# One graph layer on one core: biases copied into PSUM, projection ahead of the node updates, x added from PSUM, every second edge sum on VectorE

## The chip, the cores and the metric

One core of a Trainium2 chip. The metric is the device time of one execution in microseconds; three runs of a kernel are made and their median is told. The profile is one further execution, with the instructions of all engines.

## What is computed

512 nodes of 1024 features, 8192 edges sorted by destination. With xn = layernorm(x):

```python
feat  = concat([xn[src], xn[dst]])                     # per edge, 2048 wide
e     = relu(feat @ W_kind + b_kind)                   # 256 edges hh, 1280 oo, 6656 ho
logit = e @ W_a + b_a
alpha = exp(logit - segmax[dst]) / segsum[dst]         # softmax over each node's edges
z     = segment_sum(alpha * xn[src], dst)
gnn   = relu([xn, z] @ W_n + b_n)                      # W_hn for nodes 0..127, W_on for the rest
q, k, v = split(xn @ w_qkv + b_qkv); q = elu(q)+1; k = elu(k)+1    # 16 heads of 64
mix   = ((q @ (k^T v)) / (q . sum k)) @ w_proj + b_proj
x     = x + gnn + mix
x     = x + ffn(layernorm(x))                         # two int8/ternary-quantised layers, gelu between
```

Products with fp32 weights are made of three products each, of the parts "hi" (rounded to fp32r) and "lo" (the rest): hi x hi, hi x lo, lo x hi.

## The kernel before

**Chunks.** All weights come as chunks of 1024 x 512 (2 MB), each in two halves of 1 MB. `chunk_product` (L1468) makes one chunk's rows: for each of the two halves, for each row (128 nodes) 4 x 3 products of 128x512 into one PSUM bank. The order of the chunks is the order of everything: `HHT0, HHB0, HHT1, HHB1, K0, HN0, V0, HN1, K1, V1, Q0, Q1, ON0, ON1, PR0, PR1` after eight tables, and behind them BON0, BON1, BHN0, BHN1, which need z. A table is xn @ (half of W_ho or W_oo), four rows, and goes to DRAM; an edge's product is then a row of the source table plus a row of the destination table. HN has one row, ON three, HH two, the others four. The banks 0 to 3 are taken in turn (L402-414); `free` (L1597) waits until the bank's last reader is through.

**Bias.** A chunk in `BIASED` has a row of 512 biases. SP loads it twice (2 KB each) into `b_raw`, ScalarE makes its hi part (L654), VectorE its lo part (L884), and TensorE adds it as one more product with a row of ones, ahead of a bank's first product (`add_bias`, L1454, L1478; `first_chunk`, behind the last). These are 52 products.

**A half of weights** goes: SP loads it into `raw[h]` when VectorE is through with what lay there (`load_next`, L470); ScalarE makes the hi part (`hi_half`, L647), the first half when the chunk before last is done and the second when the first half of the chunk before is; VectorE makes the lo part (`lo_half`, L879). Both hi and lo lie in rings of three halves.

**Edges.** GpSimd gathers 68 tiles of 128 edges (L583-601): the source rows plainly, two thirds of the destination rows with an addition in the DMA; for one tile in three (`ADDED_HERE`) the destination rows go into one of two buffers (`SECOND`), and VectorE adds them (L1057). Eight slots (`SLOTS`) hold rows. `edge_tile` (L1045) on VectorE makes the relu and dot product (L1063), the mask (L1075) and the running maximum (L1087). `TILES` says how many tiles VectorE takes in each chunk, before and after the next chunk's first `lo_half`.

**Attention.** K, V and Q go through ScalarE's `positive_part` and VectorE's `add_kq`; k^T v (`kv_product`), the denominators (`den8`, `invert_den`) and `attend` are made at places of `KV_AT`, `DEN8` and `ATTEND`. Heads 0 to 7 are attended in Q1, heads 8 to 15 in ON0. PR0 and PR1 multiply the result with w_proj; ScalarE copies their banks into one of two staging slots, GpSimd adds x there (L612), SP stores them (`mix_out`).

**After the edges** GpSimd makes the maximum over partitions (L604), then PR's additions, then the lo parts of xn (L615), which ScalarE's `xn_hi` (L785) precedes. VectorE takes 36 of the edge maxima in PR1 (L1185), the exponents, and then for each tile three one-hot matrices (L1242-1244) which TensorE multiplies (L1628, L1629) into a 512 x 512 matrix A. A is transposed, z made, then ON's and HN's second halves, and the last stage with the MLP.

Every engine runs its own list in order, and so does SP, which waits for VectorE ahead of each load and for the reader ahead of each store.

Of the kernel before, what the change touches and what calls it, by code (L numbers as in the profile page):

```python
# [5 lines left out]
F32 = mybir.dt.float32  # L6
# [55 lines left out]
for _c in range(CHUNKS):  # L62
# [14 lines left out]
ADDED_HERE = [t for t in range(T_GATHERED) if t % 3 == 2]  # L77
# [14 lines left out]
ATTEND = {(Q1, 1, 0): [(0, 0), (0, 1)], (Q1, 1, 1): [(0, 2), (0, 3)], (ON0, 1, 0): [(1, 0), (1, 1)], (ON0, 1, 2): [(1, 2), (1, 3)]}  # L92
DEN8 = {(Q1, 0, 2): 0, (ON0, 0, 1): 1}
KV_AT = {(HN1, 0, 0): 0, (Q0, 0, 0): 1}


def build(nc, x, src, dst, wt, bias_rows, bq, w_a, b_a, ln1_g, ln1_b, w1, b1, ln2_g, ln2_b, w2, b2, out):
# [108 lines left out]
    b_raw = sb("b_raw", [P, CW], F32, at_braw)  # L206
# [3 lines left out]
    b_hl = sb("b_hl", [P, 2, CW], F32R, at_bhl)  # L210
# [7 lines left out]
    rz = sb("rz", [P, N], F32, at_braw)[64:72, :]  # L218
    sel8 = sb("sel8", [P, 4, P], F32R, at_bhl)
# [4 lines left out]
    ones_b = sb("ones_b", [64, P], F32R)  # L224
    ones_r = sb("ones_r", [P, P], F32R)
# [58 lines left out]
    bias_hi_done = sem("bias_hi_done")  # L284
    bias_lo_done = sem("bias_lo_done")
# [139 lines left out]
    def _(sp):  # L425
# [31 lines left out]
        sp.wait_ge(dve_consts, 1)  # L457
        load_bias(0)
# [5 lines left out]
        sp.wait_ge(bias_lo_done, 1)  # L464
        load_bias(1)
# [1331 lines left out]
```

## Time and profile before

| | |
|---|---|
| median of 3 runs | 788.03 us (785.34 to 793.8) |
| the profiled execution | 790.62 us, span 788.9 us |
| busy, share of the span | PE 668.7 us (85%), DVE 533.0 (68%), ACT 212.0 (27%), POOL 261.7 (33%) |
| granted TensorE clock, mean | 0.912 |
| DMA | 163.4 MB, 207 GB/s over the span |

PE is TensorE's products, PEld its weight loads, DVE VectorE, ACT ScalarE, POOL GpSimd; SP issues most transfers. Products are pipelined: a product of 512 columns has a row of about 0.39 us, but they start every 0.23 us, so the distance of starts is their price.

### The profile page before, as it was taken

The page shows a single profiled execution, that of the slowest core. Times are in us where ns is not written, and L with a number is a line of the kernel's source. Part 1 is how long each engine was busy: PE and PEld are TensorE (multiplying, and loading weights), DVE is VectorE, ACT ScalarE, POOL GpSimd, SP SyncE. Part 2 cuts the span into 40 slices and gives each one's busy share as a digit, 9 for nine tenths or more (in the row PEclk, how much of TensorE's full clock was granted, in tenths as well). Part 3 has the DMA queues.
Part 4 walks back from the last instruction along what each step waited for, and adds up shares of the span by engine and source line. Part 5 has one row for each costly group of instructions (what it writes and reads, how often), then busy time and mean ns, then how long its engine had stood idle before and what let it go on. Part 6 is the DMA issues. An engine that isn't in the chain of part 4 may idle for free.

```text
span 788.9 us, 8358 instructions
## 1 busy us (share of the span) xinstructions
PE 668.7 (85%) x2739; PEld 469.2 (59%) x2741; DVE 533.0 (68%) x1106; ACT 212.0 (27%) x266; POOL 261.7 (33%) x191
## 2 busy tenths in 40 slices
PE   4999999999989989999999988991917677798952
PEld 3778887788777666877886555761601011586621
DVE  7878814566287876847758676851688887327996
ACT  3232232213322443343352623211220010320101
POOL 3000308475156373736753033614250000002340
PEclk9999999999999998999999989995955768999985
DMA  9544539999989989989999183981450023140202
GB/s 348 215 160 160 184 137 306 365 339 338 332 247 352 354 239 321 298 290 310 323 324 276 55 264 106 321 267 44 156 226 1 0 64 150 54 138 6 107 27 80
DMA packets 41722, 163.40 MB, mean 207 GB/s; under 512 B 5168, under 2 KB 5552, under 8 KB 34512
## 3 DMA queue, kind: packets, MB, share of 16 engines
q0 software_dynamic: 20160, 73.41, 32.0%
q1 hardware_dynamic: 20800, 88.88, 30.2%
q10 hardware_dynamic: 720, 0.59, 0.2%
q8 instruction: 22, 0.36, 0.2%
q14 instruction: 20, 0.16, 0.1%
HBM read 146.08 MB, written 16.78 MB: 206 GB/s over the span
## 4 chain that ended last, share of the span: by engine, by line
PE 45%; DVE 26%; DMA 13%; issue 8%; ACT 3%; DVEq 2%; POOL 2%; SPq 0%; ACTq 0%; POOLq 0%
PE bank_low L1429 12%; PE bank_low L1430 11%; PE bank_low L1431 11%; DMA w_raw<-in_wt 6%; DMA gathered_rows<-edge_tables,src_row 3%; DMA edge_tables<-stage 3%; DVE w_lo L887 3%; DVE gathered_rows L1063 2%; DVEq L1042 2%; DVE hot_hi L1243 2%; DVE hot_src L1242 2%; PE bank_low L1455 2%; DVE hot_lo L1244 2%; PE bank_high L1628 1%; DVE thrown_away L1185 1%
## 5 line engine op out<-in xcount | busy, mean ns | idle before, releaser
L1429 PE MATMUL bank_low<-w_hi,xT_hi 128*128 128x512 f32 x484 | 196.9, 407 | 10.3 <-DVE w_lo L887 7.9
L1430 PE MATMUL bank_low<-w_lo,xT_hi 128*128 128x512 f32 x484 | 191.7, 396 | 0.0
L1431 PE MATMUL bank_low<-w_hi,xT_lo 128*128 128x512 f32 x484 | 191.2, 395 | 0.0
L887 DVE TENSOR_TENSOR w_lo<-w_raw,w_hi 128x2048 fp32r<-128x2048 f32 x48 | 110.0, 2291 | 65.0 <-ACT w_hi L660 63.2
L660 ACT ACTIVATE w_hi<-w_raw 128x2048 fp32r<-128x2048 f32 x49 | 93.7, 1912 | 183.0 <-DMA w_raw<-in_wt 118.5
L1429 PEld LDWEIGHTS bank_low<-w_hi,xT_hi 128*128 128x128 f32 x484 | 92.6, 191 | 39.7 <-issue 12.9
L577 POOL DMA_INDIRECT gathered_rows<-edge_tables,dst_row x46 | 88.9, 1933 | 59.7 <-DMA gathered_rows<-edge_tables,src_row 52.1
L1431 PEld LDWEIGHTS bank_low<-w_hi,xT_lo 128*128 128x128 f32 x484 | 92.7, 192 | 20.0
L577 POOL DMA_INDIRECT gathered_rows<-edge_tables,src_row x68 | 85.1, 1251 | 57.5 <-DVE gathered_rows L1063 20.8
L1430 PEld LDWEIGHTS bank_low<-w_lo,xT_hi 128*128 128x128 f32 x484 | 92.7, 192 | 18.1
L1063 DVE SCALAR_TENSOR_TENSOR gathered_rows<-gathered_rows,wa_bc 128x1024 f32<-128x1024 f32 x68 | 83.4, 1226 | 15.3 <-DMA gathered_rows<-edge_tables,dst_row 13.5
L1628 PE MATMUL bank_high<-hot_src,hot_hi 128*128 128x512 f16 x68 | 36.3, 534 | 41.2 <-DVE hot_lo L1244 32.7
L622 POOL TENSOR_TENSOR small<-small,nhalf 128x1 f32<-128x1 f32 x12 | 10.7, 890 | 169.1 <-DVE small L1323 156.2
L577 POOL DMA_INDIRECT gathered_dst<-edge_tables,dst_row x22 | 28.7, 1306 | 109.6 <-DVE gathered_rows L1057 107.5
L1628 PEld LDWEIGHTS bank_high<-hot_src,hot_hi 128*128 128x128 f16 x68 | 7.1, 104 | 86.1 <-issue 85.9
L683 ACT ACTIVATE stage<-bank_low 128x512 f32<-128x512 f32 x48 | 27.9, 594 | 109.1 <-PE bank_low L1431 41.9
L1455 PE MATMUL bank_low<-b_hl,ones_b 64*128 64x512 f32 x52 | 26.3, 506 | 18.0 <-ACT stage L683 17.9
L1629 PE MATMUL bank_high<-hot_src,hot_lo 128*128 128x512 f16 x68 | 36.6, 539 | 0.0
L1075 DVE TENSOR_SCALAR other_node<-iota,dst_f 128x128 bf16<-128x128 f16 (+1 forms) x70 | 17.9, 257 | 26.1 <-issue 26.0
L1242 DVE TENSOR_SCALAR hot_src<-iota,src_f 128x512 f16<-128x512 f16 x70 | 26.5, 379 | 7.1 <-PE bank_high L1629 6.5
L1455 PEld LDWEIGHTS bank_low<-b_hl,ones_b 64*128 64x128 f32 x52 | 9.6, 185 | 35.9 <-ACT stage L683 19.9
L1087 DVE SCALAR_TENSOR_TENSOR running_max<-other_node,logit,running_max 128x128 bf16 (+1 forms) x70 | 25.2, 360 | 3.6 <-DVE gathered_rows L1063 2.8
(277 smaller groups left out, 1016.2 us busy)
## 6 DMA issues: line engine op xcount, KB each, us to landing
w_raw<-in_wt SPq DMA_DIRECT2D x54, 1024.0 KB, 8.0
edge_tables<-stage SPq DMA_DIRECT2D x32, 256.0 KB, 3.8
x_in<-in_x SPq DMA_DIRECT2D x4, 512.0 KB, 9.1
xn_scratch<-xn SPq DMA_DIRECT2D x4, 512.0 KB, 4.5
node_top<-stage SPq DMA_DIRECT2D x8, 256.0 KB, 2.7
x_part<-in_x SPq DMA_DIRECT2D x8, 256.0 KB, 10.2
mix_out<-stage SPq DMA_DIRECT2D x8, 256.0 KB, 2.0
xn_raw<-xn_scratch SPq DMA_DIRECT2D x4, 512.0 KB, 5.9
```

What stands on the lines that cost most here:

```text
L577: pool.indirect_dma_start(dest, None, table_d[0:nodes, :], bass.IndirectOffsetOnAxis(ap=index[:, t:t + 1].bitcast(U32), axis=0), compute_o ...
L660: act.activation(w_half(c, h)[0], raw[:, h, :], ACT.Copy).then_inc(w_hi_done, 1)
L683: act.activation(stage[:, slot, :], bank[b][:, :], ACT.Copy).then_inc(evac_done, 1)
L887: dve.tensor_tensor(lo, raw[:, h, :], f32(hi), ALU.subtract).then_inc(w_lo_done, 1)
L1063: dve.scalar_tensor_tensor(out=row, in0=row, scalar=0.0, in1=wa_bc[:, :], op0=ALU.max, op1=ALU.mult, accum_out=logit[:, t:t + 1]).then_inc ...
L1242: dve.tensor_scalar(hot_src[:, s, :], iota[:, :], src_f[:, t:t + 1], None, ALU.is_equal).then_inc(hot_done, 1)
L1429: pe.matmul(dest, lh, rh, start=start and i == 0, stop=False)
L1430: pe.matmul(dest, lh, rl, start=False, stop=False)
L1431: last = pe.matmul(dest, ll, rh, start=False, stop=last_one)
L1455: return pe.matmul(bank[b][:, :], ones_b[:, :], b_hl[0:64, bias_no(c) % 2, :], start=start, stop=stop)
L1628: pe.matmul(out, hot_hi[:, t % 2, 0:P], hot_src[:, t % 2, :], start=False, stop=True, skip_group_check=True)
L1629: pe.matmul(out, hot_lo[:, t % 2, 0:P], hot_src[:, t % 2, :], start=False, stop=True, skip_group_check=True).then_inc(hot_used, 1)
```

## The change

- The bias is no product. SP loads the row once, broadcast to 128 partitions (256 KB), and ScalarE copies it into each bank before the chunk's products (`seed`); TensorE's products all accumulate (`start=False`), and `free` waits for `seeded`.
- The chunks' order is now `HHT0, HHB0, HHT1, HHB1, K0, V0, K1, V1, Q0, Q1, HN0, PR0, PR1, HN1, ON0, ON1`. The tables come bottom halves first, and the bias is in the second pair (`WEIGHTS`, `BIAS_ROW`). Heads 8 to 15 are attended in PR0.
- VectorE adds x to PR0's and PR1's banks from PSUM into the staging slots (`add_x`); ScalarE doesn't copy them.
- VectorE adds 34 of 68 tiles instead of 22. `TILES` starts a chunk earlier and ends in PR0; the 36 maxima are taken in ON0 and ON1.
- xn is read back in HN1, and its hi and lo parts are made in ON0 by ScalarE and VectorE. The one-hot loop waits for ON1's banks instead of PR1's.

```diff
+WEIGHTS = [2, 3, 0, 1, 6, 7, 4, 5, 8, 9, 10, 11, 12, 14, 16, 17, 18, 19, 13, 22, 23, 15, 20, 21, 24, 25, 26, 27]
+BIAS_ROW = {2: 0, 3: 1, 6: 2, 7: 3, HHT0: 4, HHT1: 5, K0: 6, HN0: 7, V0: 8, HN1: 9, K1: 10, V1: 11, ON0: 12, ON1: 13, PR0: 14, PR1: 15}
-TILES = {5: (2, 3), 6: (2, 2), 7: (3, 2), HHT0: (1, 1), HHB0: (1, 2), HHT1: (1, 1), HHB1: (1, 1),
-         K0: (3, 2), HN0: (0, 1), V0: (2, 3), HN1: (0, 1), K1: (2, 2), V1: (3, 2), Q0: (2, 3), Q1: (2, 2),
-         ON0: (2, 2), ON1: (1, 2), PR0: (2, 6)}
+TILES = {4: (0, 1), 5: (3, 2), 6: (3, 2), 7: (2, 3), HHT0: (2, 1), HHB0: (1, 1), HHT1: (1, 2), HHB1: (1, 1),
+         K0: (3, 2), V0: (3, 2), K1: (3, 3), V1: (2, 3), Q0: (3, 2), Q1: (5, 2), HN0: (2, 0), PR0: (4, 3)}
-MAXIMA = {PR1: (0, 36)}
+LAST_EDGES = PR0
+MAXIMA = {ON0: (0, 18), ON1: (18, 36)}
-ADDED_HERE = [t for t in range(T_GATHERED) if t % 3 == 2]
+ADDED_HERE = [t for t in range(T_GATHERED) if t % 2]
-ATTEND = {(Q1, 1, 0): [(0, 0), (0, 1)], (Q1, 1, 1): [(0, 2), (0, 3)], (ON0, 1, 0): [(1, 0), (1, 1)], (ON0, 1, 2): [(1, 2), (1, 3)]}
-DEN8 = {(Q1, 0, 2): 0, (ON0, 0, 1): 1}
-KV_AT = {(HN1, 0, 0): 0, (Q0, 0, 0): 1}
+ATTEND = {(Q1, 1, 0): [(0, 0), (0, 1)], (Q1, 1, 1): [(0, 2), (0, 3)], (PR0, 0, 1): [(1, 0), (1, 1)], (PR0, 0, 2): [(1, 2), (1, 3)]}
+DEN8 = {(Q1, 0, 2): 0, (HN0, 1, 0): 1}
+KV_AT = {(K1, 0, 0): 0, (Q0, 0, 0): 1}
...
+    seeds = {}
+    for c in BIASED:
+        for i in range(len(ROWS[c])):
+            pc, pi = bank_free[c, i]
+            key = (c - 1, -1) if pc < c - 1 else (c - 1, len(ROWS[pc]) if pc in HH + (PR0, PR1) else pi)
+            seeds.setdefault(key, []).append((c, i))
...
+        def load_bias(c):
+            if c in BIASED:
+                sp.wait_ge(seeded, seeds_to(c)) if seeds_to(c) else None
+                sp.dma_start(bias_bc[:, :], bias_rows[BIAS_ROW[c], 0].partition_broadcast(P)).then_inc(bias_loaded, 16)
...
+        for c in range(TABLES, BON0):
+            if c < ON1:
+                load_next(c + 2, 0)
+            load_bias(c + 1)
+            if c in (PR0, PR1):
+                load_x_part(c)
+            if c == HN1:
+                sp.wait_ge(prod_ready, FIRST[HN1] + HEAD)
+                for m in range(MT):
+                    sp.dma_start(xn_raw[:, m, :], xn_d[m]).then_inc(xnr_loaded, 16)
             if c in STORED:
...
+            if c < ON1:
+                load_next(c + 2, 1)
...
         pool.wait_ge(edge_max, UT)
+        pool.wait_ge(att_psum, KT)
         pool.partition_all_reduce(m_bc[:, :], run[:, :], P, RMAX).then_inc(max_done, 1)
-        for c in (PR0, PR1):
-            for i in range(MT):
...
-                pool.tensor_tensor(stage[:, s, :], stage[:, s, :], x_part[:, i, :], ALU.add).then_inc(x_added, 1)
-        for k in range(KT):
-            pool.wait_ge(xn_hi_done, k + 1)
-            pool.tensor_tensor(xn_lo[k][:, :, :], xn_raw[:, :, k * P:(k + 1) * P], f32(xn_hi[k][:, :, :]), ALU.subtract).then_inc(xn_lo_done, 1)
...
+        def seed(c, i):
+            for nc_, ni in seeds.get((c, i), ()):
+                act.wait_ge(bias_loaded, 16 * (BIASED.index(nc_) + 1))
+                act.wait_ge(*was_read(*bank_free[nc_, ni]))
+                act.activation(bank[bank_of[nc_, ni]][:, :], bias_bc[:, :], ACT.Copy).then_inc(seeded, 1)
...
-            if c != PR1:
+            if c == PR0:
+                for j in range(4):
+                    attend(1, j)
+            if c != ON1:
                 hi_half(c + 1, 1)
             if c == Q1:
                 for j in range(4):
                     attend(0, j)
-            if c == ON0:
-                for j in range(4):
-                    attend(1, j)
+            seed(c, -1)
...
+                seed(c, i)
+            if c in HH + (PR0, PR1):
+                seed(c, len(ROWS[c]))
+            if c == ON0:
+                act.wait_ge(xnr_loaded, 16 * MT)
+                act.wait_ge(edge_dot, T_GATHERED)
+                for k in range(KT):
+                    act.activation(xn_hi[k][:, :, :], xn_raw[:, :, k * P:(k + 1) * P], ACT.Copy).then_inc(xn_hi_done, 1)
...
+        def add_x(c, i):
+            s, b = stored_no(c) + i, bank_of[c, i]
+            dve.wait_ge(prod_ready, FIRST[c] + i + 1 + HEAD)
+            dve.wait_ge(x_part_loaded, 16 * MT * (1 + int(c == PR1)))
+            dve.wait_ge(stage_stored[s % 2], 16 * (s // 2))
+            dve.tensor_tensor(stage[:, s % 2, :], bank[b][:, :], x_part[:, i, :], ALU.add).then_inc(x_added, 1)
...
-            if c in (Q1, ON0):
-                a = int(c == ON0)
-                invert_den(a)
+            if c == Q1:
+                invert_den(0)
+            if c == PR0:
+                invert_den(1)
             lo_half(c + 1, 0)
...
-            if c == PR0:
+            if c in (PR0, PR1):
+                for i in range(MT):
+                    add_x(c, i)
+            if c == LAST_EDGES:
                 catch_up()
             if c in MAXIMA:
                 take_maxima(*MAXIMA[c])
+            if c == ON0:
+                for k in range(KT):
+                    dve.wait_ge(xn_hi_done, k + 1)
+                    dve.tensor_tensor(xn_lo[k][:, :, :], xn_raw[:, :, k * P:(k + 1) * P], f32(xn_hi[k][:, :, :]), ALU.subtract).then_inc(xn_lo_done, 1)
```

## Rows read from the trace of the kernel before

**Rows 1.** The page: busy times, and TensorE and DMA in 40 slices.

```profile
PE 668.7 (85%) x2739; PEld 469.2 (59%) x2741; DVE 533.0 (68%) x1106; ACT 212.0 (27%) x266; POOL 261.7 (33%) x191
...
PE   4999999999989989999999988991917677798952
...
DMA  9544539999989989989999183981450023140202
```

**Rows 2.** Busy time of each engine by stretch; then clock, DMA share, GB/s.

```profile
115.00:205.00 90.00, 90.00 (x386) 71.17 (x385) 50.65 (x73) 25.78 (x28) 55.01 (x38) 1.00 1.00 332
268.00:411.00 143.00, 137.53 (x599) 107.36 (x600) 101.15 (x157) 58.83 (x74) 80.79 (x53) 0.98 0.97 304
411.00:446.00 35.00, 35.00 (x130) 22.56 (x128) 24.98 (x35) 14.41 (x21) 7.85 (x7) 1.00 0.71 212
446.00:569.00 123.00, 98.93 (x358) 68.14 (x358) 73.49 (x141) 29.96 (x37) 41.56 (x27) 0.88 0.59 184
```

**Rows 3.** Timeline of TensorE around a bias product (start, duration, instruction).

```profile
483.10 0.39 PE L1431 MATMUL bank_low<-w_hi,xT_lo 128*128 128x512 f32 x1
483.42 0.50 PE L1455 MATMUL bank_low<-b_hl,ones_b 64*128 64x512 f32 x1
...
484.42 0.40 PE L1431 MATMUL bank_low<-w_hi,xT_lo 128*128 128x512 f32 x1
```

**Rows 4.** Timeline: starts of K0, HN0, V0; ScalarE reads Q0's last bank.

```profile
264.46 0.50 PE L1455 MATMUL bank_low<-b_hl,ones_b 64*128 64x512 f32 x1
...
288.84 0.50 PE L1455 MATMUL bank_low<-b_hl,ones_b 64*128 64x512 f32 x1
...
302.54 0.49 PE L1455 MATMUL bank_low<-b_hl,ones_b 64*128 64x512 f32 x1
...
410.86 0.69 ACT L718 ACTIVATE tmp<-bank_low,nbq 128x512 f32<-128x512 f32 x1 [0.79 <-PE bank_low L1431]
```

**Rows 5.** Groups of VectorE by line and shape (busy, mean ns, idle before).

```profile
L887 DVE TENSOR_TENSOR w_lo<-w_raw,w_hi 128x2048 fp32r<-128x2048 f32 x48 | 110.0, 2291 | 65.0 <-ACT w_hi L660 63.2 <-issue 1.1
...
L1063 DVE SCALAR_TENSOR_TENSOR gathered_rows<-gathered_rows,wa_bc 128x1024 f32<-128x1024 f32 x68 | 83.4, 1226 | 15.3 <-DMA gathered_rows<-edge_tables,dst_row 13.5
...
L1057 DVE TENSOR_TENSOR gathered_rows<-gathered_rows,gathered_dst 128x1024 f32<-128x1024 f32 x22 | 26.8, 1219 | 0.0
...
L1087 DVE SCALAR_TENSOR_TENSOR running_max<-other_node,logit,running_max 128x128 bf16 x68 | 23.7, 349 | 3.5 <-DVE gathered_rows L1063 2.8
...
L1075 DVE TENSOR_SCALAR other_node<-iota,dst_f 128x128 bf16<-128x128 f16 x68 | 17.3, 254 | 26.0 <-issue 26.0
```

**Rows 6.** The gathers' DMA queue in 118-446 us; waits (total, times, longest).

```profile
q0 software_dynamic: 16848, 61.35, 64.1%
...
POOL gathered_dst L577 <- DVE gathered_rows L1057: 107.5, 15, 23.4
```

**Rows 7.** Timeline of VectorE: attention of heads 8 to 15, first and last.

```profile
457.96 3.34 DVE L1164 RECIPROCAL rz<-rz 8x512 f32<-8x512 f32 x1
...
479.50 0.69 DVE L1157 TENSOR_TENSOR oT_lo<-qT,oT_hi 128x512 fp32r<-128x512 f32 x1 [0.70 <-ACT oT_hi L739]
```

**Rows 8.** Timeline of GpSimd, ScalarE and TensorE at the end of PR0.

```profile
544.58 2.47 POOL L612 TENSOR_TENSOR stage<-stage,x_part 128x512 f32<-128x512 f32 x2 [7.54 <-issue]
...
547.95 0.60 ACT L683 ACTIVATE stage<-bank_low 128x512 f32<-128x512 f32 x1 [27.90 <-DMA mix_out<-stage]
...
548.60 0.79 PE L1455 MATMUL bank_low<-b_hl,ones_b 64*128 64x512 f32 x1 [17.86 <-ACT stage L683]
```

**Rows 9.** Timeline: first one-hot product, and VectorE in the loop.

```profile
579.97 0.60 PE L1628 MATMUL bank_high<-hot_src,hot_hi 128*128 128x512 f16 x1 [9.96 <-DVE hot_lo L1244]
...
580.93 1.39 DVE L1242 TENSOR_SCALAR hot_src<-iota,src_f 128x512 f16<-128x512 f16 x1
...
590.95 0.34 DVE L1242 TENSOR_SCALAR hot_src<-iota,src_f 128x512 f16<-128x512 f16 x1
```

**Rows 10.** Group of VectorE: the 36 maxima taken in PR1.

```profile
L1185 DVE SCALAR_TENSOR_TENSOR other_node<-iota,dst_f,max_bc 128x128 bf16<-128x128 f16 x36 | 12.6, 405 | 8.7 <-issue 8.2 <-DVE other_node L1185 0.5
```

More of the change, by code:

```diff
@@ L49 @@
 TABLES = 8
-(HHT0, HHB0, HHT1, HHB1, K0, HN0, V0, HN1, K1, V1, Q0, Q1, ON0, ON1, PR0, PR1,
+(HHT0, HHB0, HHT1, HHB1, K0, V0, K1, V1, Q0, Q1, HN0, PR0, PR1, HN1, ON0, ON1,
  BON0, BON1, BHN0, BHN1) = range(TABLES, TABLES + 20)
 CHUNKS = TABLES + 20
-BIASED = [c for c in range(TABLES) if c % 4 < 2] + [HHT0, HHT1, K0, HN0, V0, HN1, K1, V1, ON0, ON1, PR0, PR1]
-STORED = list(range(TABLES)) + [HN0, HN1, ON0, ON1, PR0, PR1]
+WEIGHTS = [2, 3, 0, 1, 6, 7, 4, 5, 8, 9, 10, 11, 12, 14, 16, 17, 18, 19, 13, 22, 23, 15, 20, 21, 24, 25, 26, 27]
+BIAS_ROW = {2: 0, 3: 1, 6: 2, 7: 3, HHT0: 4, HHT1: 5, K0: 6, HN0: 7, V0: 8, HN1: 9, K1: 10, V1: 11, ON0: 12, ON1: 13, PR0: 14, PR1: 15}
+BIASED = sorted(BIAS_ROW)
+STORED = list(range(TABLES)) + [HN0, PR0, PR1, HN1, ON0, ON1]
 HH = (HHT0, HHB0, HHT1, HHB1)
@@ L391, in use_of @@
         return USES.index((kind, a, j))
-    def bias_no(c):
-        return sum(b < c for b in BIASED)
     def evac_no(c, i):
-        return FIRST[c] + i + 1 - sum(len(ROWS[b]) for b in HH if b < c)
-    bank_of, bank_free, last = {}, {}, {}
+        return FIRST[c] + i + 1 - sum(len(ROWS[b]) for b in HH + (PR0, PR1) if b < c)
+    bank_of, bank_free, owner = {}, {}, {}
     turn = 0
@@ L412, in build, with was_read, seed_no, seeds_to @@
                 turn += 1
-                bank_free[c, i] = last.get(b)
-                last[b] = ("act", evac_no(c, i))
+                bank_free[c, i] = owner.get(b)
+                owner[b] = (c + 1 if c in HH else c, i)
+    def was_read(c, i):
+        if c in HH:
+            return hh_read, 2 * (c == HHB1) + i + 1
+        if c in (PR0, PR1):
+            return x_added, MT * (c == PR1) + i + 1
+        return evac_done, evac_no(c, i) + HEAD
+    seeds = {}
[4 more added lines that the diff above has]
+            seeds.setdefault(key, []).append((c, i))
+    seed_order = [row for key in sorted(seeds) for row in seeds[key]]
+    def seed_no(c, i):
+        return seed_order.index((c, i)) + 1
+    def seeds_to(c):
+        return sum(len(ROWS[b]) for b in BIASED if b < c)
     def stored_no(c):
@@ L481, in _ @@
             load_next(c + 2, 1)
-        for c in range(TABLES, PR1):
-            load_next(c + 2, 0)
-            if c == PR0:
-                load_x_part(PR0)
+        for c in range(TABLES, BON0):
+            if c < ON1:
+                load_next(c + 2, 0)
+            load_bias(c + 1)
+            if c in (PR0, PR1):
[4 more added lines that the diff above has]
+                    sp.dma_start(xn_raw[:, m, :], xn_d[m]).then_inc(xnr_loaded, 16)
@@ L504, in _ @@
         for s in range(2):
[L505 removed]
+            sp.wait_ge(stage_stored[s], 16 * (stored_no(ON1 + 1) // 2))
         sp.wait_ge(xn_lo_done, KT)
@@ L1186, in take_maximum @@
                                      op0=ALU.is_equal, op1=ALU.mult, accum_out=mx_e[:, t:t + 1]).then_inc(mx_gathered, 1)
-        for c in range(TABLES, PR1 + 1):
+        def add_x(c, i):
[4 more added lines that the diff above has]
+            dve.tensor_tensor(stage[:, s % 2, :], bank[b][:, :], x_part[:, i, :], ALU.add).then_inc(x_added, 1)
+        for c in range(TABLES, ON1 + 1):
             if c == HHT0:
@@ L1636, in _ @@
         pe.matmul(bank[7][:, :], zeros[:, :], iota[:, :], start=False, stop=True, skip_group_check=True).then_inc(A_psum, 1)
-        pe.wait_ge(evac_done, evac_no(PR1, 3) + HEAD)
+        pe.wait_ge(evac_done, evac_no(ON1, 2) + HEAD)
+        pe.wait_ge(evac_done, evac_no(HN1, 0) + HEAD)
         for b in range(NB):
```

120 lines of the change are left out of this document (33 added, 87 removed).

## The prediction

> **What bounds the kernel now.** I read first the busy times and the 40 slices of the page [rows 1]: TensorE is full for most of the first two thirds, and the DMA engines are nearly as full. The stretches then say where each of them yields [rows 2]. In 115-205 us TensorE never stops at the full clock, with a DMA share of 1.00. In 268-411 us it is busy for 137.5 of 143 us beside a DMA share of 0.97, so both are near their limit, and VectorE has 101 us of work. In 446-569 us TensorE is busy for 98.9 of 123 us at a clock of 0.88, and the DMA share is only 0.59: this stretch is bound by neither, but by waits. The largest stands in rows 8. GpSimd does its all-reduce only after the last edge, so it reaches PR0's first x addition at 544.58; ScalarE waits 27.90 us for a staging slot, and TensorE 17.86 us for a bank.
>
> So four things count: TensorE's instructions up to 411 us, what the DMA engines and VectorE allow in the same time, the chain at the end of the projection, and the loop of one-hot products behind it.
>
> **The bias products.** 52 go (16 in the tables, 4 for HH, 18 for K, V and HN, 14 for ON and PR). One costs more than its row: from the last product of one row to the third of the next is 1.32 us (483.10 to 484.42) with a bias product between [rows 3]; three steps of the usual 0.23 us would be 0.69. So 0.63 us each, 33 us in all, if TensorE stays the limit. In their place come 52 ScalarE copies into PSUM, which the trace does not show. The nearest row is a copy of 512 columns out of PSUM, 0.60 us [rows 8]; the bounds are 0 and twice that, and I take 0.6: 31 us on an engine that is busy 27% of the time [rows 1] and loses 16 bias splits and 8 PR copies. In a full chunk a half row of products lasts 12 x 0.23 = 2.8 us, and ScalarE reads a bank and seeds it in 1.2 us, while TensorE comes back to it three half rows later: nothing on the path. The wait is another matter. Where a chunk's bank came free more than one chunk ago, its seed stands behind *both* halves of `hi_half` of that chunk in ScalarE's order (HHT1, the first rows of K0, three rows of PR0, three of ON0). TensorE could start a chunk on its first half alone; now it needs the second half landed as well. The bias row as a broadcast is 256 KB instead of 4 KB, 16 times: 4 MB.
>
> **Tables (to about 209 us).** 16 x 0.63 = -10. Against that: 16 edge tiles instead of 14, with their gathers, in a stretch where the DMA share is already 1.00. One tile is two gathers of 0.5 MB. I take +4 (bounds 0 and +12). Term: -6.
>
> **HH.** 4 x 0.63 = -2.5; one tile more on VectorE (about 2.8 us), and the seeds behind second halves at HHT1 and K0, together taken at 2; term +2 after rounding, bounds -4 and +9.
>
> **K0 to Q0.** Before, from 264.46 to 410.86: 146.4 us [rows 4]. HN0 and HN1 leave. HN0 takes 288.84 to 302.54, 13.7 us with its stall; HN1 24 x 0.23 + 0.63 = 6.1. 16 biases: 10. Together -30. VectorE does not let it all through. Its costs are [rows 5]: a half of weights 2.29; a tile 1.23 + 0.35 + 0.25, plus 26.0/68 = 0.38 of idle before it, 2.2; a tile whose rows it adds itself 1.22 more. With 22 of 68 added that is 2.6 a tile, with 34 it is 2.8. K0 now has five tiles (14), two halves (4.6), four additions of 0.69 and the HH finish (about 4): 25 us against TensorE's 96 x 0.23 = 22. K1 with six tiles stands at 25 too, V0 and V1 at 19, Q0 at 22. In sum VectorE has about 110 us in five chunks and TensorE 117 (five times 22 and two products of K with V), in an order that doesn't always fit: +7 lost. Term: -23 (bounds -30 and -8).
>
> What the added half gives back is in the DMA engines. In 118-446 us the gather queue moved 61.35 MB with 64.1% of the engines' time [rows 6]. What a gather that adds costs more than a plain one can't be read off, since their mix was the same throughout. I bound the saving of a converted gather by 0 and by a whole gather's mean: the 16848 packets are 117 gathers (144 packets each), and 64.1% of 328 us over 117 is 1.8 us. I take 1, so 12 us over the edges, which pays for the three tiles that now stand before Q1 and for the broadcasts. Its cost is depth: with two buffers and every second tile added here, GpSimd runs four tiles ahead and not six, and it already waited 107.5 us for that addition [rows 6]. Taken at 0, bounds in the fourth rival.
>
> **From Q1 to the first one-hot product.** Before: 410.86 to 579.97, 169 us [rows 4, 9]. After, counted from Q1's start:
> - Q1: VectorE has the half (with the end of Q0, 5 us) and five tiles (14) ahead of `invert_den`, 5.2 us, of which the reciprocal is 3.34 [rows 7]. TensorE has done four half rows, `den8` and one row by 17 us and waits for about 25. Q1 ends at 39; before it took some 31.
> - HN0: its second half waits for VectorE, which first adds Q1's four exponentials: 50. Then two tiles, the next half, and PR0's seeds behind the load of its second half: PR0 starts at 57.
> - PR0: attention for heads 8 to 15 stands here and not in ON0, and PR0's own second half needs its result. VectorE has a half, four tiles and `invert_den` first: the factors come at 75 instead of by 63. From the reciprocal to the last part of the result took 21.5 us before (457.96 to 479.50) [rows 7], with two or three half rows of products to fill it. TensorE ends PR0 at about 98; its own work since Q1's start is about 74, so some 24 us of it is waiting.
> - The last tiles are done at about the same point. PR1 22, HN1 5.5, ON0 and ON1 33, and 5 for ON0's seeds behind its second half: 164. VectorE still has 18 maxima, a half and the exponents: 36 maxima took 12.6 + 8.7 = 21.3 us [rows 10], so 18 take 10.7; xn's low parts come before them (8 x 0.7). The loop starts at about 173.
> What goes is GpSimd's part: the 17.86 us stall, and the wait of SP's stores that held the weights behind them. x added from PSUM is one VectorE operation of about 0.7 us (the nearest row, 0.69 [rows 7]), and lies behind PR's products. But what it hid is now TensorE's wait for attention. Term: +4 (bounds -20 and +15).
>
> **The one-hot loop.** From 580.93 to 590.95 two rounds took 10 us, while GpSimd made xn's low parts; VectorE's `hot_src` took 1.39 us there and 0.34 right after [rows 9]. That work is now VectorE's own, before the loop. A round without GpSimd beside it is about 1 us, so -8 (bounds -9 and 0). The Trainium skill's page SBUF — State Buffer, Who interferes with whom, says that such VectorE operations and a GpSimd instruction shut each other out of the shared port pair for a whole instruction; the trace agrees, at 1.39 against 0.34 us. By that rule GpSimd's xn work would cost the same wherever it overlapped, and the term is the same.
>
> Everything behind A's transposes is unchanged: 0.
>
> **Sum.** -6 + 2 - 23 + 4 - 8 = -31. The profiled execution took 790.62 us (span 788.9), the median of the runs is 788.03, 0.3% less. 790.6 - 31 = 759.6, less 2.6: 757 us.
>
> **Rivals.**
> (B) TensorE alone paces it. For: in 115-205 us it lost nothing at DMA share 1.00. Against: the sums for VectorE. Then -10 - 2.5 - 28 before Q1, -5 behind, -8 in the loop: -53.5, 735 us.
> (C) The DMA engines pace it up to Q0. For: shares of 1.00 and 0.97. Against: HN0 and HN1 take 4.2 MB of weights with them. Then Q1 starts only 5 us earlier, its stretch is 10 longer by the waits above, and the loop gains 8: -3, 785 us.
> (D) Slower: the two buffers for added rows. Every added tile can wait for the landing of a gather that was issued four tiles earlier. A wait of 1.5 us at each of 34 tiles is 51 us on VectorE, less the 31 gained: 808 us. It decides from 31/34 = 0.9 us a tile. For: GpSimd's 107.5 us. Against: VectorE itself waited only 13.5 us for the gathers it needed [rows 5].
>
> **Chances.** Forecast 0.53, B 0.20, C 0.17, D 0.10. Range: 735 takes in B, 781 the weak end of the forecast; C and D above it are left out together with the far end of B. The forecast's own range is 745 to 772. A measurement of this kernel can tell about 1%, 8 us, from no change. Faster by more: the forecast, B and a little of C, 0.77. Within 1%: most of C, 0.14. Slower: D, 0.09.
>
> **What would show it.** Right: no ScalarE wait for mix_out stores; K0 to Q0 in about 123 us; TensorE waits for `rz_hl` in Q1 and in PR0 of some 7 and 12 us; the first one-hot product near 557 us; rounds of 1 us from the start. Wrong: the same start of Q1 (C), VectorE waits for gathers above 45 us in sum (D), or a stretch from Q1 to the loop below 150 us (B).

## The result, and the profile after

| | before | after |
|---|---|---|
| median | 787.2 us (785.34 to 793.8) | 798.87 us (795.88 to 800.28) |
| ratio of the times | | 1.0133, interval [1.0075, 1.0191] |
| the profiled execution | 790.62 us, span 788.9 | 795.88 us, span 794.1 |
| granted TensorE clock, mean | 0.912 | 0.904 |

The changed kernel is 1.3% slower; the forecast was 757 us, and 798.87 lies above the range of 735 to 781. (A fourth run of the kernel before brings its median from 788.03 to 787.2.) The two profiled executions are 5.3 us apart and the medians 11.7, so what is read off the profiles below accounts for some 5 of the 12 us. The page of after (busy times, TensorE, its clock and the DMA engines in 40 slices):

```profile
PE 645.8 (81%) x2687; PEld 471.8 (59%) x2689; DVE 533.2 (67%) x1113; ACT 229.0 (29%) x294; POOL 221.3 (28%) x175
...
PE   4999999898786899599994747995966656798962
...
PEclk9999999999997899799997966998997779999895
DMA  8554649999989985998988398267450014140201
```

TensorE lost 23 us of busy time against [rows 1] as meant, but where its row stood at 8 or 9 for most of the first two thirds there are now holes, and in the deepest of them the clock's row falls too: from 20 us to the first one-hot product the mean granted clock was 0.96 before and is 0.92. The stretches (engines, then clock, DMA share, GB/s), against [rows 2]:

```profile
115.00:205.00 90.00, 84.93 (x371) 69.60 (x371) 52.36 (x79) 26.97 (x31) 50.22 (x39) 0.98 1.02 349
205.00:268.00 63.00, 48.66 (x198) 38.81 (x197) 45.39 (x64) 19.41 (x16) 30.09 (x21) 0.86 0.94 324
268.00:411.00 143.00, 131.55 (x599) 109.21 (x598) 97.11 (x159) 58.69 (x81) 70.94 (x54) 0.94 0.92 291
411.00:446.00 35.00, 25.03 (x70) 13.25 (x69) 22.03 (x32) 6.52 (x9) 11.02 (x8) 0.80 0.59 176
446.00:569.00 123.00, 94.03 (x341) 68.27 (x340) 73.51 (x122) 42.24 (x51) 21.87 (x15) 0.86 0.65 214
```

The waits of after (total, times, longest) name who made the holes. ScalarE's wait is for the bias row's transfer, and TensorE's for ScalarE's copy of it:

```profile
ACT bank_low L684 <- DMA bias_bc<-in_bias_rows: 54.3, 10, 14.0
...
PE bank_low L1443 <- ACT bank_low L684: 34.1, 6, 9.5
...
PE bank_high L1601 <- DVE rz_hl L1162: 15.6, 2, 10.0
...
PE bank_low L1443 <- DVE w_lo L885: 12.3, 5, 7.0
...
PE bank_low L1443 <- issue: 8.1, 1, 8.1
```

The last line is a seed too: PR0's, right behind ScalarE's copy:

```profile
475.08 1.64 ACT L684 ACTIVATE bank_low<-bias_bc 128x512 f32<-128x512 f32 x3 [7.92 <-DMA bias_bc<-in_bias_rows]
475.78 0.76 PE L1443 MATMUL bank_low<-w_hi,oT_hi 128*128 128x512 f32 x1 [8.05 <-issue]
```

So TensorE stood some 42 us for seeds, in seven stalls. The timelines (start, duration, instruction, idle before) of TensorE, ScalarE, VectorE and of SP's queue, at the steps of the prediction:

```profile
273.30 0.77 PE L1443 MATMUL bank_low<-w_hi,xT_hi 128*128 128x512 f32 x1 [3.33 <-ACT bank_low L684]
...
305.64 11.71 SPq L448 DMA_DIRECT2D w_raw<-in_wt  x2
317.39 0.43 SPq L453 DMA_DIRECT2D bias_bc<-in_bias_rows  x1
...
327.29 0.60 ACT L684 ACTIVATE bank_low<-bias_bc 128x512 f32<-128x512 f32 x1 [14.03 <-DMA bias_bc<-in_bias_rows]
...
328.04 0.77 PE L1443 MATMUL bank_low<-w_hi,xT_hi 128*128 128x512 f32 x1 [8.12 <-ACT bank_low L684]
...
403.56 0.69 ACT L721 ACTIVATE tmp<-bank_low,nbq 128x512 f32<-128x512 f32 x1 [0.79 <-PE bank_low L1445]
...
430.85 2.07 PE L1601 MATMUL bank_high<-qT,kvb 128*128 128x512 f32 x2 [9.97 <-DVE rz_hl L1162]
...
489.39 2.07 PE L1601 MATMUL bank_high<-qT,kvb 128*128 128x512 f32 x2 [5.59 <-DVE rz_hl L1162]
...
552.27 0.77 PE L1443 MATMUL bank_low<-w_hi,xT_hi 128*128 128x512 f32 x1 [8.04 <-ACT bank_low L684]
...
594.80 0.60 PE L1635 MATMUL bank_high<-hot_src,hot_hi 128*128 128x512 f16 x1 [6.58 <-DVE hot_lo L1259]
...
595.76 0.35 DVE L1257 TENSOR_SCALAR hot_src<-iota,src_f 128x512 f16<-128x512 f16 x1
596.74 0.35 DVE L1257 TENSOR_SCALAR hot_src<-iota,src_f 128x512 f16<-128x512 f16 x1
```

Read K1's seed from below: TensorE waits 8.12 us at 328.04 for the copy at 327.29; that waited for a transfer which SP issued only at 317.39. SP had stood in L448, the load of the next weights, whose condition is VectorE's `w_lo`, and in its program the bias load stands behind it. The bias was 10 us on its way.

With the landmarks of [rows 4, 9] the four terms can be read off (the last is the span less the first one-hot product):

| stretch | before | after | difference | predicted |
|---|---|---|---|---|
| to K0's first product | 264.46 | 273.30 | +8.8 | -4 |
| K0 to Q0's last bank | 146.40 | 130.26 | -16.1 | -23 |
| from there to the first one-hot product | 169.11 | 191.24 | +22.1 | +4 |
| loop and rest | 208.9 | 199.3 | -9.6 | -8 |

The last line is the loop alone: from the start of its first to that of its last product it takes 91.7 us before (579.97 to 671.66) and 82.1 after (594.80 to 676.93).

### The profile page after: what moved, and what is told of

Read it like the earlier page. It is cut to its first block, busy times and chain, and to the rows that moved or that the text cites. A ratio compares the mean times of both kernels' runs of the same rounds, so it can differ in the third digit from the quotient of the medians.

```text
span 794.1 us, 8278 instructions
## 1 busy us (share of the span) xinstructions
PE 645.8 (81%) x2687; PEld 471.8 (59%) x2689; DVE 533.2 (67%) x1113; ACT 229.0 (29%) x294; POOL 221.3 (28%) x175
## 3 DMA queue, kind: packets, MB, share of 16 engines
q0 software_dynamic: 20160, 73.41, 30.2%
## 4 chain that ended last, share of the span: by engine, by line
PE 44%; DVE 27%; DMA 16%; issue 6%; ACT 4%; DVEq 2%; POOL 1%; SPq 0%; ACTq 0%; POOLq 0%
PE bank_low L1443 12%; PE bank_low L1444 11%; PE bank_low L1445 11%; DMA bias_bc<-in_bias_rows 7%; DVE w_lo L885 5%; DMA edge_tables<-stage 4%; DMA gathered_rows<-edge_tables,dst_row 2%; DVE gathered_rows L1059 2%; DMA w_raw<-in_wt 2%; DVE hot_src L1257 2%; DVEq L1038 2%; DVE hot_hi L1258 2%; PE bank_high L1601 1%; DVE hot_lo L1259 1%; DVE thrown_away L1181 1%
## 5 line engine op out<-in xcount | busy, mean ns | idle before, releaser
L1444 PE MATMUL bank_low<-w_lo,xT_hi 128*128 128x512 f32 x484 | 193.9, 401 | 0.0
L1445 PE MATMUL bank_low<-w_hi,xT_lo 128*128 128x512 f32 x484 | 193.6, 400 | 0.0
L1059 DVE SCALAR_TENSOR_TENSOR gathered_rows<-gathered_rows,wa_bc 128x1024 f32<-128x1024 f32 x68 | 83.3, 1225 | 36.5 <-DMA gathered_rows<-edge_tables,dst_row 32.9
L587 POOL DMA_INDIRECT gathered_rows<-edge_tables,src_row x68 | 85.8, 1262 | 41.0 <-DMA edge_tables<-stage 20.6
L587 POOL DMA_INDIRECT gathered_dst<-edge_tables,dst_row x34 | 36.0, 1060 | 151.4 <-DVE gathered_rows L1053 149.6
L587 POOL DMA_INDIRECT gathered_rows<-edge_tables,dst_row x34 | 61.2, 1800 | 15.3 <-issue 8.5
L1635 PE MATMUL bank_high<-hot_src,hot_hi 128*128 128x512 f16 x68 | 31.9, 469 | 35.0 <-DVE hot_lo L1259 29.6
L684 ACT ACTIVATE bank_low<-bias_bc 128x512 f32<-128x512 f32 x52 | 30.6, 598 | 68.6 <-DMA bias_bc<-in_bias_rows 54.3
L1053 DVE TENSOR_TENSOR gathered_rows<-gathered_rows,gathered_dst 128x1024 f32<-128x1024 f32 x34 | 41.5, 1220 | 0.0
L677 ACT ACTIVATE stage<-bank_low 128x512 f32<-128x512 f32 x40 | 23.6, 594 | 54.3 <-PE bank_low L1445 32.0
L1443 PE MATMUL bank_low<-w_hi,oT_hi 128*128 128x512 f32 x64 | 26.9, 420 | 8.1 <-issue 8.1
L1636 PE MATMUL bank_high<-hot_src,hot_lo 128*128 128x512 f16 x68 | 32.7, 481 | 0.0
```

Of the source, the lines that this page charges most:

```text
L587: pool.indirect_dma_start(dest, None, table_d[0:nodes, :], bass.IndirectOffsetOnAxis(ap=index[:, t:t + 1].bitcast(U32), axis=0), compute_o ...
L684: act.activation(bank[bank_of[nc_, ni]][:, :], bias_bc[:, :], ACT.Copy).then_inc(seeded, 1)
L1053: dve.tensor_tensor(row, row, dst_rows[:, n % SECOND, :], ALU.add).then_inc(row_added_here, 1)
L1059: dve.scalar_tensor_tensor(out=row, in0=row, scalar=0.0, in1=wa_bc[:, :], op0=ALU.max, op1=ALU.mult, accum_out=logit[:, t:t + 1]).then_inc ...
L1443: pe.matmul(dest, lh, rh, start=start and i == 0, stop=False, skip_group_check=True)
L1444: pe.matmul(dest, lh, rl, start=False, stop=False, skip_group_check=True)
```

## The experiments

All ratios are to runs of the kernel before on the same chip; each interval is 95%. The median of the kernel before lies between 787.2 and 790.21 us in these groups of runs, so a difference of under 3 us between medians of two groups says nothing by itself.

**1. The bias load ahead of the weights'.** In both of SP's loops:

```diff
-            load_next(c + 2, 0)
             load_bias(c + 1)
+            load_next(c + 2, 0)
```

> The changed kernel with one edit: SP issues a chunk's bias load ahead of the next load of weights, which waits for VectorE, and not behind it. Theory T (the seeds wait for a bias load that is issued late and lands 7 to 10 us after its issue): TensorE's idle time that ends with a seed falls from 42 us (34.1 us by name and 8.1 us put down to issue at PR0) to some 20, and the time falls from 799 to about 785. Rival O (the order, with heads 8 to 15 attended inside PR0, is what costs): the seeds' waits turn into waits for VectorE, the time stays within 4 us. Rival S (34 sums on VectorE instead of 22 cost it): no change.

Measured: 781.45 us, ratio 0.9905 [0.9869, 0.9941]. Moving one line gives 17.5 us and turns the sign: now 1% faster than before. TensorE's waits for seeds by name fell to 16.4 us in five (20 were expected). Its landmarks: K0's first product at 261.84 (-2.6 against before), K0 to Q0's last bank 126.1 (-20.3), from there to the first one-hot product 190.5 (+21.4), the rest 199.8 (-9.1). So the late load explains the first two stretches, which come within 3 us of the prediction, and next to nothing of the third. There its waits show this instead:

```profile
PE bank_high L1601 <- DVE rz_hl L1162: 29.7, 2, 17.6
```

and the timeline of TensorE and VectorE, where:

```profile
415.19 2.07 PE L1601 MATMUL bank_high<-qT,kvb 128*128 128x512 f32 x2 [12.10 <-DVE rz_hl L1162]
...
469.30 1.22 DVE L1059 SCALAR_TENSOR_TENSOR gathered_rows<-gathered_rows,wa_bc 128x1024 f32<-128x1024 f32 x1 [4.99 <-DMA gathered_rows<-edge_tables,dst_row]
...
475.85 2.07 PE L1601 MATMUL bank_high<-qT,kvb 128*128 128x512 f32 x2 [17.55 <-DVE rz_hl L1162]
```

In PR0 TensorE no longer waits 8.05 us for its seed, and waits 17.55 us for the factors instead of 5.59: the one wait had covered part of the other.

**2 and 3. No biases at all, in either kernel.** In the changed kernel the copies, their waits and the loads are left out; in the one before the 52 products, the splits and the loads.

> The changed kernel without biases of the chunks (they are left out of the result): no seeds, no bias loads; TensorE waits for a bank's last reader alone. T: the 42 us of seed waits and about 5 us at the low clock behind them go, some of it returns as waits for VectorE: 755 to 765. O or S: the time that the seeds cost is small beside the other waits, 780 or more.

> The kernel before without biases (left out of the result): no bias products, loads and splits. This is the most that taking 52 products off TensorE can bring in the old order. If TensorE paces the kernel: 52 x 0.63 = 33 us less, 755. If the DMA engines and VectorE are next behind it: half of that, 770. T and O differ in e2 minus e3: T expects e2 at or below e3, O expects e2 above e3 by 10 us or more.

Measured: 771.4 us, ratio 0.9751 [0.9699, 0.9803], and 776.17 us, ratio 0.9827 [0.9767, 0.9886]. The first lies between its two ranges, the second above both of its values; the changed kernel's is 5 us lower, which rules out O's 10 us the other way, but the intervals overlap. The second is the surprise. The prediction priced the 52 products at 33 us; to leave them out of the kernel before, and put nothing in their place, brings 14. Where the rest went, its stretches show (columns as above):

```profile
115.00:205.00 90.00, 89.32 (x401) 73.52 (x399) 44.65 (x67) 21.38 (x22) 51.60 (x37) 1.00 1.04 342
205.00:268.00 63.00, 54.45 (x235) 43.74 (x235) 49.28 (x71) 21.20 (x16) 29.62 (x19) 0.92 0.97 326
```

and the timeline of TensorE, one row of the kernel before (HHT0's first product) and then those without biases:

```profile
209.50 0.50 PE L1455 MATMUL bank_low<-b_hl,ones_b 64*128 64x512 f32 x1
...
198.47 0.48 PE L1411 MATMUL bank_low<-w_hi,feat_src_hi 128*128 128x512 f32 x1
...
211.54 0.80 PE L1411 MATMUL bank_low<-w_hi,feat_src_hi 128*128 128x512 f32 x1 [7.21 <-DVE w_lo L871]
...
531.59 0.80 PE L1411 MATMUL bank_low<-w_hi,oT_hi 128*128 128x512 f32 x1 [20.75 <-ACT stage L671]
...
566.69 0.61 PE L1606 MATMUL bank_high<-hot_src,hot_hi 128*128 128x512 f16 x1 [15.57 <-DVE hot_lo L1226]
```

In the tables nothing is lost: HHT0 starts at 198.47 for 209.50, so 16 products fewer bring 11.0 us (16 x 0.63 = 10), at a DMA share of 1.04. The other 36 bring 5 of their 23 us. HHT0's second half waits 7.21 us for `w_lo`, and in 205-268 us TensorE is busy for 54.45 us (58.01 before) at a clock of 0.92 (0.97). TensorE's waits for `w_lo` rise from 12.8 to 20.0 us in all, ScalarE's for the landing of weights from 118.5 to 167.0, VectorE's for gathered rows from 13.5 to 30.9: with TensorE faster, the transfers and VectorE's parts come due. From K0's first product to Q0's last bank it is 140.3 us for 146.4; from Q0's last bank (396.81) to the first one-hot product it takes 169.9 us, as before (169.1), though 14 of the bias products stood there: the waits grew by what the products gave. Experiments 1 and 2 also say what the seeds still cost with the load moved: 781.45 against 771.4, 10 us, where the prediction had taken almost nothing.

**4. Fewer sums on VectorE, in the changed kernel.**

```diff
-ADDED_HERE = [t for t in range(T_GATHERED) if t % 2]
+ADDED_HERE = [t for t in range(T_GATHERED) if t % 3 == 2]
```

> The changed kernel with VectorE adding one tile in three again (22 instead of 34). T: within 5 us of the changed kernel, since 15 us of VectorE's work goes and the DMA engines get 12 more gathers with addition. S: faster by 8 us or more, with fewer waits of VectorE for gathers (32.9 us now).

Measured: 795.12 us, ratio 1.0067 [1.0038, 1.0096]: some 4 us below the changed kernel, with overlapping intervals. The sums are no great part of the loss, and VectorE's waits for gathers stay (34.4 us).

**5. The tiles behind the attention.** On experiment 1:

```diff
-Q1: (5, 2), HN0: (2, 0), PR0: (4, 3)}
+Q1: (2, 3), HN0: (2, 2), PR0: (0, 4), PR1: (1, 2)}
-LAST_EDGES = PR0
+LAST_EDGES = PR1
```

> The changed kernel with bias loads first (781.45 us), and its edge tiles placed otherwise: Q1 (2,3) for (5,2), HN0 (2,2) for (2,0), PR0 (0,4) and PR1 (1,2) for (4,3). There VectorE reached its reciprocal only after five and four tiles, and TensorE waited 29.7 us for rz_hl in two places. Theory O (the tiles ahead of the reciprocal cost it): the rz_hl waits fall below 10 us in sum and the time to about 765. Rival: the edges have to be done anyway before the maxima, and VectorE is the pace from Q1 to the loop; then the waits move to w_lo and the banks of PR0, and the time stays at 778 to 784.

Measured: 768.11 us, ratio 0.9739 [0.9684, 0.9794]. TensorE's `rz_hl` waits, by the line's own answer:

```profile
who waited for it (us, times):
  PEld bank_high L1601: 9.0, 2
  PE bank_high L1601: 8.1, 2
```

29.7 us fell to 8.1, and from Q0's last bank to the first one-hot product it is 175.2 us for 190.5. That is the second cause: five tiles before the first reciprocal and four before the second. The rival, that the waits would only move, is out, though HN0's wait for `w_lo` grew from 7.04 to 10.33 us.

**6. Seeds ahead of the second half's split.** On experiment 5, in ScalarE's order:

```diff
+            seed(c, -1)
             if c != ON1:
                 hi_half(c + 1, 1)
             if c == Q1:
                 for j in range(4):
                     attend(0, j)
-            seed(c, -1)
```

> As e5, and in ScalarE's order the seeds of banks that are long free stand ahead of the split of the next chunk's second half instead of behind it. Theory T2 (that half's landing still holds the seeds at HHT1, K1 and ON0; 4.9 + 5.2 + 4.7 us): 8 to 12 us below e5. Rival: the seeds only hid the wait for the same half, which TensorE needs three rows later: 0 to 4 us.

Measured: 764.35 us, ratio 0.9716 [0.9646, 0.9786]. The intervals of 5 and 6 overlap; the gain of 4 us is not shown, and one of 8 to 12 is unlikely. TensorE's waits for seeds moved and did not go: 20.8 us in five in experiment 5, 20.5 in six here (HHT1 4.99 to 5.22, ON0 4.69 to 3.42, K0 a new 2.80). The one that the expectation puts at K1 is V1's third row (341.60 in experiment 1): ScalarE had itself waited 11.48 us for VectorE's sums of K and came to that bank at 339.31.

**7. Of the change only this: x added by VectorE, in the kernel before.** In the staging slot, behind ScalarE's copy; GpSimd's two loops over PR0 and PR1 go.

> The kernel before with one part of the change: x is added by VectorE (in the staging slot, behind ScalarE's copy), not by GpSimd behind its all-reduce. If the 17.86 us wait of TensorE for a bank and ScalarE's 27.9 us for mix_out were on the path: 772 to 776. If the last edges set the end of this stretch anyway (maxima and one-hot products come behind them): 784 to 788.

Measured: 790.2 us, ratio 1.0045 [1.0011, 1.0079], above both ranges. The wait of 17.86 us [rows 8] fell to 7.11, and the time did not:

```profile
532.51 0.79 PE L1454 MATMUL bank_low<-b_hl,ones_b 64*128 64x512 f32 x1 [7.11 <-ACT stage L676]
...
552.11 0.60 ACT L676 ACTIVATE stage<-bank_low 128x512 f32<-128x512 f32 x1 [2.17 <-PE bank_low L1430]
...
583.19 0.61 PE L1627 MATMUL bank_high<-hot_src,hot_hi 128*128 128x512 f16 x1 [30.23 <-DVE hot_lo L1243]
```

The projection ends 17 us earlier than before (its last bank is read at 552.11, not 569.17), and then TensorE waits 30.23 us for VectorE, which takes its 36 maxima and the exponents behind PR1's additions. This doesn't show that the stall was free, because the edit does two things. VectorE in the kernel before (two rows), and then here, up to the first of the maxima:

```profile
551.59 2.29 DVE L887 TENSOR_TENSOR w_lo<-w_raw,w_hi 128x2048 fp32r<-128x2048 f32 x1 [16.22 <-ACT w_hi L660]
553.80 0.35 DVE L1185 SCALAR_TENSOR_TENSOR other_node<-iota,dst_f,max_bc 128x128 bf16<-128x128 f16 x1
...
552.74 0.69 DVE L1217 TENSOR_TENSOR stage<-stage,x_part 128x512 f32<-128x512 f32 x1 [2.07 <-ACT stage L676]
554.47 0.35 DVE L1178 SCALAR_TENSOR_TENSOR other_node<-iota,dst_f,max_bc 128x128 bf16<-128x128 f16 x1 [1.03 <-issue]
```

Before, the late staging slots hold the maxima as well: ScalarE splits the next half only behind the bank that waited 27.90 us, and VectorE waits 16.22 us for that split with the maxima behind it. Here that wait is gone, but the additions stand in its place and wait for PR1's last bank, and the maxima start no earlier. Experiment 11 parts the two.

**8. Of the change only this: half of the sums on VectorE, in the kernel before.** The edit of 4, the other way round.

> The kernel before with one part of the change: VectorE sums every second tile's rows (34) and not every third (22). VectorE gets 12 x 1.22 = 14.6 us more, GpSimd's gathers with addition fall from 46 to 34. If the DMA engines pace the edges: 780 to 784 (12 x 1.2 us of their time). If VectorE does, or the two buffers: 790 to 800. From e4 (one in three in the changed kernel: -3.8) I expect about 792.

Measured: 788.35 us, ratio 1.0000 [0.9976, 1.0024]. No gain, no loss, where 792 was expected.

**9. Q1's sums of exponentials ahead of its tiles**, on experiment 6, with `Q1: (2, 1), HN0: (2, 3), PR0: (0, 4), PR1: (2, 2)`.

> e6 with Q1's four sums of exponentials ahead of the tiles of its second half, and those tiles later: Q1 (2,1), HN0 (2,3), PR0 (0,4), PR1 (2,2). In e6 TensorE waited 10.3 us at HN0 for w_lo, since VectorE came to Q1's sums behind three tiles, and ScalarE's two tmp slots with it. If that wait is on the path: 5 to 8 us below e6 (764.4), so 757 to 760. If VectorE's edges set the end from Q1 to the loop: 762 to 768.

Measured: 769.17 us, ratio 0.9750 [0.9718, 0.9783]. A miss: HN0's wait fell from 10.31 to 6.59 us, and the loop started 6 us later than in 6 (568.08 for 561.88).

**10. The same with a third of the sums on VectorE.**

> e9 with VectorE's sums back at every third tile (22 for 34). If VectorE's time is what counts once the waits are gone (14.6 us less work on it): 3 to 8 us below e9. If the DMA engines' time is (12 more gathers with addition): 2 to 8 above. e4 gave -3.8 in the changed kernel, e8 0.0 in the one before; I expect -2.

Measured: 761.87 us, ratio 0.9705 [0.9626, 0.9785]. The better end of what was expected, but its interval overlaps that of 9.

**11. Experiment 7 with the maxima ahead of PR1's additions.**

```diff
             if c in MAXIMA:
                 take_maxima(*MAXIMA[c])
             if c in (PR0, PR1):
                 for i in range(MT): ...
```

> e7 with VectorE's 36 maxima ahead of its x additions of PR1 and not behind them. In e7 the products ended 17 us earlier than before, and the first one-hot product came 3 us later, behind maxima and exponents. Theory (the chain from the last edge over all-reduce, maxima and exponents sets the start of the loop, and the 17.86 us stall lay beside it): first one-hot product 565 to 572 and 774 to 780 us, since only now that chain moves. If instead the products or the weights behind them bind: 786 to 790, as e7.

Measured: 782.16 us, ratio 0.9920 [0.9897, 0.9944]. In between: the maxima start at 544.80, 9 us earlier than before, and the first one-hot product comes at 576.62, 6.6 us earlier than in 7, where 11 to 18 had been expected; the time falls by 8.0 us, where 10 to 16 had been. The chain over the maxima is on the path, since its move alone pays. Against the kernel before it is 0.8%, some 6 us, for a stall that is now 5.1 us: it was not free. Now the last two banks of PR1 wait for staging slots whose additions stand behind the maxima, and the last weights behind those:

```profile
544.80 0.35 DVE L1178 SCALAR_TENSOR_TENSOR other_node<-iota,dst_f,max_bc 128x128 bf16<-128x128 f16 x1 [0.37 <-issue]
...
568.64 1.27 ACT L676 ACTIVATE stage<-bank_low 128x512 f32<-128x512 f32 x2 [15.42 <-DMA mix_out<-stage]
...
571.74 2.29 DVE L880 TENSOR_TENSOR w_lo<-w_raw,w_hi 128x2048 fp32r<-128x2048 f32 x1 [1.11 <-ACT w_hi L653]
...
576.62 0.60 PE L1627 MATMUL bank_high<-hot_src,hot_hi 128*128 128x512 f16 x1 [17.60 <-DVE hot_lo L1243]
```

**12. Experiment 6 with a third of the sums on VectorE.**

> e6 (bias loads first, tiles behind the attention, seeds ahead of the second half's split) with VectorE's sums at every third tile (22 for 34). e10 was 7 us below e9 with that one edit, e4 4 us below the changed kernel. If VectorE's time counts: 757 to 761 us, ratio about 0.963. If e10's gain was scatter: 763 to 768. Both ways it should stand below the kernel before and below the changed one.

Measured: 761.2 us (756.89 to 767.13), ratio 0.9642 [0.9607, 0.9677]. 3.6% faster than the kernel before, and 38 us below the changed one; its interval also lies below that of 5, so the edits of 6 and 12 together are a gain. That a third of the sums is better than half is not shown by any pair alone; 4, 10 and 12 all point that way (-3.8, -7.3, -3.2 us), and 8 does not.

## Why the prediction was wrong

- **"In a full chunk ... nothing on the path", the seeds.** This is the first step that failed. The two copies' time was right (0.60 us, and 0.602 was measured), and four of the seven stalls are where its list of seeds behind a second half has them (HHT1, K0, PR0, ON0). K1's is not on that list, nor are those of two tables (2.31 and 2.77 us). What was not followed is the load: it was counted as 4 MB of traffic and not as an instruction in SP's queue, behind a load that waits for VectorE's `w_lo`. The old bias was two rows of 2 KB, and its parts lay in a two-deep buffer; the new one is 256 KB in a single buffer, free only when the last seed of the chunk before is made, so it can't be fetched far ahead. Seven stalls of TensorE, 42 us, where the sum had at most 7. Worth 17.5 us in time (experiment 1), plus 10 that stay with the load moved (1 against 2).
- **33 us for 52 bias products, "if TensorE stays the limit".** The 0.63 us each is right as a price on TensorE, and in the tables it shows in full: 11.0 us for 16 (experiment 3), although the DMA share was 1.00. So that share did not say that the transfers were a limit there; it rose to 1.04. Behind the tables the condition fails: 36 products priced at 23 us bring 5, because `w_lo`, weights and gathered rows come due. In all they bring 14 us.
- **Tables and HH: -4 predicted, +8.8 after, -2.6 with the load moved.** HHT0 starts at 201.45 in experiment 1, 8.0 us earlier than before (6 were predicted), and HH takes 5.4 us more (2 were predicted). HHT1's stall alone is 9.49 us in the changed kernel and 4.86 with the load moved.
- **K0 to Q0: -23 predicted, -16.1 after, -20.3 with the load moved.** Right within its bounds; the failed part is K1's seed, 8.12 us, and with the load moved V1's third row, 5.17 us.
- **Q1 to the loop: +4 predicted, +22.1 after.** The second step that failed. The prediction's own steps, in us from Q0's last bank, with what the traces have (ON0's first product is its 98 for the end of PR0, and 22, 5.5 and 5):

| | predicted | after | experiment 1 |
|---|---|---|---|
| first factors (`rz_hl`) | 25 | 27.3 | 27.3 |
| HN0's second half | 50 | 55.5 | 55.8 |
| PR0's first product | 57 | 72.2 | 64.6 |
| second factors | 75 | 85.8 | 87.9 |
| ON0's first product | 130.5 | 148.7 | 146.8 |
| first one-hot product | 173 | 191.2 | 190.5 |

  Of the 17.5 us that experiment 1 is late at the loop, 13 are there at the second factors. VectorE comes 6 us late to PR0's part, and among the four tiles ahead of the reciprocal it waits 4.99 us for a gather. The prediction saw that the tiles stand there, but counted them without waits, and gave TensorE some 24 us of waiting up to PR0's end; with HN0's 7.04 it is 36.7 in experiment 1. The `rz_hl` waits were to be 7 and 12 us and are 12.10 and 17.55 (9.97 and 5.59 after, where PR0's seed with its 8.05 us covers part of the second). ON0's seeds were to cost 5 and cost 8.04 (4.68 with the load moved). In 411-446 us the clock was 0.80, and the work between was counted at the full one. Of the 21 us over the kernel before, 15 hang on tiles ahead of the reciprocals (experiment 5). Moving a tile is free in the sum of VectorE's work and dear in front of something TensorE waits for.
- **The 17.86 us stall.** It was one of four things the prediction said count. Mostly taken away in the kernel before it is worth 6 us net (experiment 11), and nothing when the additions go ahead of the maxima (experiment 7). The prediction didn't subtract it as such, but took the chain behind it to be shorter after the change because x no longer waited for GpSimd.
- **The loop: -8 predicted, -9.6 after.** Right, in size and in mechanism: `hot_src` takes 0.35 us, and rounds start 0.98 us apart from the first on; the loop itself is 9.6 us shorter.
- **Half of the sums: 0 net, with 12 us of DMA time back.** Near in both. The gather queue's share of the span fell from 32.0% to 30.2%, (252.4 - 239.8) / 12 = 1.05 us for each gather that no longer adds, with the whole change between the two; pairs that differ in the sums alone give 0.6 to 1.0. The time does not follow (experiments 4 and 8).
- **The rivals.** None was what happened. C comes near by its sign: Q1 started 7.3 us earlier where C had 5 and the forecast 27; but the cause was the bias load, since experiment 1 brings it to 22.9 with the same transfers. D had the direction and the wrong mechanism: VectorE's waits for gathers rose from 13.5 to 32.9 us, below the 45 that the prediction named. In the faster experiment 1 they are 48.8 and in experiment 12, with a third of the sums, 47.3, so they go with the pace and not with the sums, which are worth 0 to 7 us. Slower had a chance of 0.09 because only D was asked for it; that the seed's load could wait in SP's queue was in the diff to see.

What stays open: of the +21 us between Q0 and the loop in experiment 1, some 6 are not traced (175.2 us in experiment 5, 169.1 before); and what the order of the chunks is worth alone, since no run has it without the other parts. The two kernels without biases differ by 5 us for all parts but the biases together, with overlapping intervals.

## What to carry to other kernels

Where a small operand moves from one engine to another, follow its transfer too: which queue issues it, what that queue waits for just ahead of it, and how many buffers it has. Before a removed instruction is priced at its duration, leave it out of the kernel before and time that; here it was worth 14 us and not 33. And a wait of the busiest engine is worth what the chain that ends last gains by its going: the 17.86 us were worth 6 net, and 0 where the work that took the wait away stood ahead of that chain (experiments 11 and 7). Take such a wait away alone before a change is built on it, and look at what the edit puts in front of the next thing that is waited for.

## What the runs showed of the hardware

- In the changed kernel seven waits of 3.33 to 9.49 us stand before products of 512 columns between 200 and 560 us, and behind each of them TensorE came back at the lower of its two clock levels (1.2 for 2.4 GHz): a product row of 0.76 to 0.80 us, then 0.63, and starts 0.43 us apart where 0.23 is usual, as here at K1. Behind the wait of 2.77 us at 182.23 the starts stayed 0.23 us apart.

```profile
328.60 0.63 PE L1444 MATMUL bank_low<-w_lo,xT_hi 128*128 128x512 f32 x1
329.03 0.63 PE L1445 MATMUL bank_low<-w_hi,xT_lo 128*128 128x512 f32 x1
329.45 0.63 PE L1443 MATMUL bank_low<-w_hi,xT_hi 128*128 128x512 f32 x1
```

  The granted clock was 0.54 from 328.0 to 334.5 us and 1.00 from 337 to 345. So a stall of 8.12 us cost more than itself: each product that follows at that pace costs 0.2 us more.
- A gather of 0.5 MB that adds took 0.6 to 1.0 us more of the 16 DMA engines' time than a plain one, in four pairs that differ in 12 of them: 252.4 us into 243.9 in the kernel before (31.1% of 784.3, experiment 8), 251.9 (31.8% of 792.2, experiment 4) into 239.8 in the changed one, 247.7 (experiment 10) into 240.3 (experiment 9), 250.3 (experiment 12) into 239.9 (experiment 6).
- A broadcast row of 256 KB was 7.1 to 9.9 us from issue to use at a DMA share of 0.99 to 1.03 (317.39 to 327.29 for K1, 263.01 to 272.55 for K0, 467.99 to 475.08 for PR0, in the changed kernel).
- A copy of 128x512 f32 by ScalarE from SBUF into a PSUM bank took 0.602 us (52 of them, 0.580 to 0.605), as long as one out of PSUM (0.60 [rows 8]).
